# Attention with keys on the partitions, row maxima by a pass of their own, and fp32 probabilities times V

## The reference, cut to what matters

```
q, k, v = (h @ W).reshape(b, s, 16, 64)        # q and k rotated by position
logits  = einsum('bhqd,bhkd->bhqk', q, k)
logits  = where(causal, logits, -1e9) / 8
attn    = softmax(logits, axis=-1)
out     = einsum('bhqk,bhkd->bhqd', attn, v) @ Wo
x       = x + layernorm(out)
```

## Time and profile before

| | |
|---|---|
| median of 3 runs | 3296.17 us (3294.3 to 3298.45) |
| the profiled execution, its own time | 3296.03 us |
| its span, first to last instruction | 3294.2 us |
| PE busy | 2897.0 us (88%) |
| VectorE busy | 2390.9 us (73%) |
| ScalarE busy | 2022.5 us (61%) |
| GpSimd busy | 121.6 us (4%) |

### The profile page before, as it was taken

The page is one execution under the profiler, slowest core; times in us unless marked ns, Lnnn a source line. Parts: engine busy times, 40 slices in busy tenths (PEclk is TensorE's granted clock), DMA queues, the critical chain, the costliest instruction groups (busy, mean ns, idle before and its releaser), DMA issues. The chain is left out here.

```text
span 3294.2 us, 58839 instructions
## 1 busy us (share of the span) xinstructions
PE 2897.0 (88%) x17856; PEld 1547.4 (47%) x17856; DVE 2390.9 (73%) x4289; ACT 2022.5 (61%) x4003; POOL 121.6 (4%) x397
## 2 busy tenths in 40 slices
PE   4989999688888888985883699999999999999996
PEld 2534444466666666663441244444444444444442
DVE  6535555688888888884556787787777777777767
ACT  1114443688888888882214767676676676676742
POOL 0000000000000000000002000000000000000002
PEclk9999999899999999997996899999999999999998
DMA  4322222201010101102112111111111111111124
GB/s 164 116 77 58 76 76 64 72 22 40 22 41 22 40 22 35 27 5 86 64 70 69 53 52 49 50 52 52 46 52 49 50 52 45 53 46 52 52 71 153
DMA packets 77773, 188.88 MB, mean 57 GB/s; under 512 B 12304, under 2 KB 12688, under 8 KB 77200
## 3 DMA queue, kind: packets, MB, share of 16 engines
q1 hardware_dynamic: 77456, 185.13, 17.7%
HBM read 151.52 MB, written 33.55 MB: 56 GB/s over the span
## 5 line engine op out<-in xcount | busy, mean ns | idle before, releaser
L1234 PE MATMUL gp<-region,wgu 128*128 128x512 f16 x4224 | 931.3, 383 | 89.3 <-DVE wgu L1392 89.3
L1271 ACT ACTIVATE line<-code,offsets 128x512 f32<-128x512 f32 x1056 | 697.2, 713 | 111.3 <-DVE below L1370 45.7
L1234 PEld LDWEIGHTS gp<-region,wgu 128*128 128x128 f16 x4224 | 416.0, 99 | 600.9 <-issue 110.9
L786 ACT ACTIVATE probs<-logits,nbias,coef 128x512 f32<-128x512 f32 (+3 forms) x640 | 461.0, 720 | 100.4 <-POOL nbias L719 86.4
L1247 PE MATMUL yp<-wd,inter 128*128 128x512 f16 x2112 | 463.9, 380 | 24.5 <-DVE wd L1392 17.4
L835 DVE SCALAR_TENSOR_TENSOR pt_pair<-tp,pt_pair 128x512 f16<-128x512 f32 (+3 forms) x640 | 385.8, 603 | 76.2 <-ACT pt_pair L795 72.4
L736 PE MATMUL logits<-k_sb,q_sb 128*128 128x512 f16 (+3 forms) x1280 | 347.3, 354 | 104.6 <-ACT probs L786 61.2
L819 DVE TENSOR_REDUCE mx<-logits 128x1 f32<-128x512 f32 (+3 forms) x640 | 383.9, 600 | 33.7 <-PE logits L736 33.1
L795 ACT ACTIVATE pt_pair<-tp 128x512 f16<-128x512 f32 (+3 forms) x640 | 343.4, 537 | 25.2 <-PE tp L749 21.0
L749 PE MATMUL tp<-ident,probs 128*128 128x128 f32 x2176 | 349.2, 276 | 4.3 <-DVE pt_pair L835 2.7
L548 PE MATMUL pq<-region,wt_pair 128*128 128x512 f16 x1536 | 333.4, 380 | 14.9 <-DVE wt_pair L599 14.9
(11 more groups left out here) (107 smaller groups left out, 2823.0 us busy)
## 6 DMA issues: line engine op xcount, KB each, us to landing
qk_pairs<-r_pair SPq DMA_DIRECT2D x128, 128.0 KB, 2.1
k_sb<-qk_pairs SPq DMA_DIRECT2D x64, 256.0 KB, 5.4
cst<-in_gate_codes SPq DMA_DIRECT2D x44, 256.0 KB, 2.6
sst<-in_gate_scales SPq DMA_DIRECT2D x88, 128.0 KB, 2.9
cst<-in_up_codes SPq DMA_DIRECT2D x44, 256.0 KB, 2.7
sst<-in_up_scales SPq DMA_DIRECT2D x88, 128.0 KB, 3.1
cst<-in_down_codes SPq DMA_DIRECT2D x44, 256.0 KB, 2.7
sst<-in_down_scales SPq DMA_DIRECT2D x88, 128.0 KB, 3.0
```

Source lines behind the costliest of these rows:

```text
L786: a.activation(probs[:, g0 % P_RING, 0:w * P], sp_[:, g0 % S_RING, 0:w * P], ACT.Exp, bias=nbias[:, m:m + 1], scale=col(coef, 0), accum_ou ...
L1234: mm = pe.matmul(gp[:, e % 2, m, :], wgu[:, par, m, a, col0:col0 + P], xnT[:, b, k, tok], start=(k == 0 and a == b), stop=(k == KT - 1 and ...
L1271: a.activation(line[:, k % 4, :], code7[:, :], ACT.Identity, scale=slope, bias=offsets[:, k:k + 1]).then_inc(s_L.sem, 1)
```

## The change

Stages 1, 3 and 4 change.

- **Stage 1**: V is kept as one fp32 number. `v_hi` becomes `v_out`, which writes fp32 on ScalarE; `v_lo` is gone. A 65th column of ones stands beside the 64 of each head (`DV = D + 1`), set by one VectorE memset at the start of stage 3.
- **Stage 3** has two passes over a head. The first (`item`, `maximum`) makes the logits with queries on the partitions, with q_hi, q_lo and k_hi alone (one matmul a chunk in place of two), only for the maxima. When the 40 chunks of a head are through, one small reduce, one transpose, one ScalarE copy and two DMAs (to HBM, and from there to 64 partitions) put the negated maxima into rows 64 to 127 of `q2`. The second pass (`scores`, 27 slots behind the first) makes the logits with keys on the partitions, in groups of four pieces of 128 keys by 256 queries. Its second matmul holds k_lo in rows 0 to 63 and a constant in rows 64 to 127, so it also subtracts the maxima. ScalarE takes exp of a whole group (up to 1024 columns, no bias, no row sum). Two slots later `times_v` multiplies each 128x128 square of fp32 probabilities with 65 columns of fp32 V in one instruction; the ones column gives the row sum. VectorE divides each pair of output tiles by it. The turning of the squares, their hi and lo parts, GpSimd's bias and `o_lo` are gone. A head now has 20 groups and 20 slots.
- **Stage 4**: `on` is gone, and the transposes read `o_rows` itself. TensorE's list is written out instead of looped.

```
-        LAG_EXP, LAG_T, LAG_PV = 4, 6, 8
+        CHUNK = 2 * P
+        GROUP = 4 * CHUNK
+        for k in range(NI):
+            per_slot[k * (NGH - 1) // NI].append(k)
+        XLEAD, LAG_PV, P_RING = NGH + 7, 2, 4
...
+                def spread_max(t, u):
+                    sp.wait_ge(s_m.sem, s_m.done(t * 2 + u))
+                    sp.dma_start(m_dram[u], m16[:, u, :]).then_inc(d_ms.sems[u], 16)
+                    sp.wait_ge(d_ms.sems[u], d_ms.done(t + 1))
+                    sp.dma_start(q2[D:P, u, :], m_dram[u:u + 1].rearrange("a t p -> a (t p)").to_broadcast([D, S])
...
+                        pe.matmul(bank, k1[:, u, keys], q1[:, u, q0:q0 + w], start=True, stop=False)
+                        mm = pe.matmul(bank, k2[:, u, keys], q2[:, u, q0:q0 + w], start=False, stop=not diagonal)
...
+                    mm = pe.matmul(sx[:, b, 0:w], xq[:, u, qt * P:(qt + 1) * P], xk[:, u, c * CH:c * CH + w],
+                                   start=True, stop=not diagonal)
...
-                        pe.matmul(op[:, :], pt_pair[:, g0 % PT_RING, 0, at], v_at,
-                                  start=(kt == 0), stop=False)
-                        mm = pe.matmul(op[:, 0:D], pt_pair[:, g0 % PT_RING, 1, at], v_hi_at,
-                                       start=False, stop=(kt == qt))
+                            mm = pe.matmul(ob[:, m % 2, tile * CHUNK:tile * CHUNK + DV],
+                                           probs[:, n0(u, g) % P_RING, c0:c0 + P], v_at,
...
                 def slot(at):
+                    x, z, w = at(0), at(XLEAD), at(XLEAD + LAG_PV)
+                    if z:
+                        scores(*z)
+                    if x:
+                        t, u, q = x
+                        for k in per_slot[q]:
+                            item(t, u, k)
+                    if w:
+                        times_v(*w)
+                    if x and x[2] == NGH - 1:
+                        turn_max(x[0], x[1])
...
+                    a.activation(probs[:, n0(u, g) % P_RING, 0:w], st3[:, n0(u, g) % 2, 0:w], ACT.Exp,
+                                 scale=col(coef, 0)).then_inc(s_P.sem, 1)
...
+                        v.reciprocal(rinv[:, m % 2, :].unsqueeze(2), b[:, :, D:DV]).then_inc(s_rv.sem, 1)
+                        v.wait_ge(s_rv.sem, s_rv.done(tile))
+                        v.tensor_tensor(o_rows[:, 2 * m:2 * m + 2, bass.ds((t * 2 + u) * D, D)], b[:, :, 0:D],
...
-                def v_lo(i, u):
-                    v.wait_ge(s_vhi.sem, s_vhi.done(i))
...
-                    if st.has(2, ST):
-                        i = st.item(2)
-                        v.wait_ge(s_t4.sem, s_t4.room(i))
-                        v.tensor_tensor(on[:, :].rearrange("p (h d) -> p h d", d=D),
```

More of the change, by code:

```diff
@@ L28 @@
 SC = S // CH
+DV = D + 1
 GW = 2 * P
@@ L629, in build @@
         c2.close()
[L639 to L649, removed]
@@ L699, in _, with both, part, load_max @@
             def _(sp):
-                with sp.Fori(0, HEADS // 2) as t:
+                def both(which, head):
+                    return qk_dram[which, bass.ds(head, 1)].rearrange("a b r s -> (a b r) s")
+                def part(which, head, n):
+                    return qk_dram[which, bass.ds(head, 1), n].rearrange("a r s -> (a r) s")
+                def load_max(head, u):
+                    sp.dma_start(xq[:, u, :], both(0, head)).then_inc(d_X.sems[u], 16)
+                    for copy in range(2):
+                        sp.dma_start(xk[copy * D:(copy + 1) * D, u, :], part(1, head, 0)).then_inc(d_X.sems[u], 16)
@@ L722, in _ @@
             @block.tensor
             def _(pe):
-                for s in (s_QK, s_PT, s_PV):
+                for s in (s_S, s_PV):
                     pe.sem_inc(s.sem, s.credit)
-                def logits(t, g0, g):
-                    m, c = place[g0]
-                    (u, qt), w = tiles[m], width(m, c)
-                    if m % (NT // 2) == 0 and c == 0:
-                        pe.wait_ge(d_q.sems[u], d_q.done(t))
-                    pe.wait_ge(s_P.sem, s_P.room(g))
-                    bank = sp_[:, g0 % S_RING, 0:w * P]
-                    diagonal = c == chunks[m] - 1
-                    for part in range(2):
-                        mm = pe.matmul(bank, q_sb[:, u, qt * P:(qt + 1) * P],
-                                       k_sb[:, u, part, c * CH:c * CH + w * P],
-                                       start=(part == 0), stop=(part == 1 and not diagonal))
-                    if diagonal:
-                        mm = pe.matmul(sp_[:, g0 % S_RING, (w - 1) * P:w * P], ident_bf[:, :],
-                                       mask_bf[:, :], start=False, stop=True)
-                    mm.then_inc(s_QK.sem, 1)
@@ new lines, in turn_max, with times_v @@
+                def turn_max(t, u):
+                    head = t * 2 + u
+                    pe.wait_ge(s_nm.sem, s_nm.done(head))
+                    pe.transpose(sx[0:ST, (u * NX + NI) % 2, 0:P], nm[:, u, :], ident[:, :]).then_inc(s_T.sem, 1)
+                def times_v(t, u, g):
+                    m, first, last, pieces = groups3[g]
+                    n = (t * 2 + u) * NGH + g
+                    pe.wait_ge(s_P.sem, s_P.done(n))
+                    if first:
+                        pe.wait_ge(s_o.sem, s_o.room((t * 2 + u) * NQ + (NQ - 1 - m)))
+                    c0 = 0
+                    for kt, q0, w in pieces:
+                        v_at = v_rows[:, kt, bass.ds(t * 2 + u, 1), :].rearrange("p a c -> p (a c)")
+                        for j in range(w // P):
+                            tile = (q0 + j * P - m * CHUNK) // P
+                            mm = pe.matmul(ob[:, m % 2, tile * CHUNK:tile * CHUNK + DV],
+                                           probs[:, n0(u, g) % P_RING, c0:c0 + P], v_at,
+                                           start=(first and c0 == 0), stop=(kt == 2 * m + tile),
+                                           skip_group_check=True)
+                            c0 += P
@@ L809, in _ @@
+                for u in range(2):
+                    a.sem_inc(d_ms.sems[u], 16)
                 slots(a, slot)
@@ L853, in _ @@
+                def slot(at):
+                    x, w = at(0), at(XLEAD + LAG_PV)
+                    if x:
+                        t, u, q = x
+                        for k in per_slot[q]:
+                            maximum(t, u, k)
+                        if per_slot[q] and per_slot[q][-1] == NI - 1:
+                            row_maxima(t, u)
+                    if w:
+                        output(*w)
                 slots(v, slot)
```

335 lines of the change are left out of this document (168 added, 167 removed).

## The result

| | before | changed |
|---|---|---|
| median, us | 3296.14 (3294.3 to 3298.45, 4 runs) | 3340.28 (3337.0 to 3340.98, 4 runs) |
| profiled execution: span, us | 3294.2 | 3339.2 |
| ratio to before | | 1.0133, 95% 1.0119 to 1.0147 |

The change makes the kernel slower by 44 us, 1.3%, well outside the interval of the ratio. The prediction was 3067, its range 3040 to 3295. It missed both.

The account below looks back on a forecast made before the run. Stage 3 was taken as bound by the coupling of three nearly full engines, stages 1 and 5 by PE. 3296.0 - 205 (stage 3) - 4 (its first load) - 3.4 (stage 1) - 17 (stage 4) = 3067 us, range 3040 to 3295.

Parts of the forecast that it names:

- V is 2176 fp32 instructions of 65 columns, t each: Stage 3, TensorE: probabilities times V, with t the time per instruction, taken as 0.115 us, 250 us in all.
- Its half about passes: Stage 3, fp32 product with V: the 65 columns pass four times, 0.110 us per instruction.
- Its half about loads: Stage 3, fp32 product with V: two weight loads of 0.06 us each (0.12) are hidden beside the passes.
- The load sets the distance: Rival, stage 3: 0.109 us between transposes is the load's time; two loads give 0.218, 224 us more, 3291; chance 0.07.
- The start: Start of stage 3: 33 us until the first scores, in which PE works 11.4 and idles 21.
- the other matmuls with their waits: Stage 3 without V, behind its start: 395 us (386 of matmuls, less 11.4 at the start, plus 20 of waits).
- Loads not hidden (slower): Rival, stage 3: an fp32 instruction's loads can't overlap its matmuls; 0.236 us each, 263 us more, 3330; chance 0.12.
- The first L538: End of stage 1: without V's lower part in VectorE's way, the barrier to stage 2 opens 3.4 us earlier.
- The shorter first load: Start of stage 3: 1 MB for head 0's maxima comes first, about 6 us instead of 10, less by 4.
- Stage 4 gave 17.5 for 17: Stage 4: an instruction leaves VectorE's chain, which sets the period; less by 14.7 + 2.4 = 17 us.
- VectorE's waits in short groups: Stage 3, end of each head: PE waits for VectorE's two reduces and an output, some 1.3 us a head, 20 in all.
- if starts of L814 stand 0.2 us apart: Sign of a wrong prediction, stage 3: fp32 instructions with V starting 0.2 us apart, where 0.115 was assumed.

Follow-up runs that it names:

- the narrow transposes: Changed kernel with every fp32 square but the first of each group replaced by one fp32 transpose, 128 weight columns, 64 columns passing; V left out there: 3080.51 us.
- the interleaved order: Changed kernel with the scores' f16 matmuls and the fp32 squares of probabilities times V alternating in each slot of stage 3, nothing left out: 3288.05 us, ratio 0.9972.
- four products: Changed kernel with probabilities and V as single f16, lower parts left out, and each square's product taken four times: 3141.32 us, ratio 0.9529.
- one product: Changed kernel with probabilities and V as single f16, lower parts left out, and one f16 matmul per square: 2924.62 us, ratio 0.887.

## Why the prediction was wrong

**The step that failed** is the term "V is 2176 fp32 instructions of 65 columns, t each", with t = 0.115. Its half about passes was right (0.110 us per square). Its half about loads, "two loads of 0.06 lie beside it, since loads are hidden in the earlier trace rows", was wrong in size: a load is 0.112, twice what passes beside it, so it sets the distance. Measured t = 0.220, V 479.5 us instead of 250, 229.5 us more. The 0.06 was read rightly from a transpose, and the narrow transposes confirm it; it isn't the load of an fp32 matmul. The text said that no fp32 matmul but transposes stood in the trace, and still carried a number over the very difference.

**The rival that came true** was "The load sets the distance", at 0.218 and a chance of 0.07; the earlier trace rows had been counted against it, and against the rule of the Trainium skill that says the same. It gave 3291, the time came out at 3340. The 49 us between are the sum's other errors, measured apart in the changed kernel:

- *Turns of the loop*: 27.5 us in six gaps, nothing in the sum. In the kernel before, six turns of up to 3.0 us cost 16.7; here six waits cost 25.9, and 44 in the interleaved order.
- *The start*: 38.4 us to the first scores instead of 33, at a granted clock of 0.50, the 1.2 GHz level; PE had stood idle for 17 us before it.
- *The clock behind the turns*: the other matmuls with their waits take 407 us behind the start, 395 in the sum; 29 of them stand at the 1.2 GHz level and would take half at the other. That leaves nothing for waits that the sum had too low.
- *t itself*: 0.220 for 0.218, 5 us.

**"Loads not hidden (slower)"** named nearly the right time, 3330, by a mechanism that doesn't occur: with 130 columns passing, the distance is still 0.112, so load and pass lie side by side. A chance given to its figure would have been right by luck.

**What held.** The first L538 starts at 239.26 instead of 242.61, 3.3 for 3.4. The shorter first load gave 4.1 for 4. Stage 4 gave 17.5 for 17. VectorE's waits in short groups, 20 in the sum, came 28 times from 640 us on, 14.7 us of PE's idle time and 28.8 of its loads' (59.6 with the first head's). VectorE stayed under 420 us busy and ScalarE under 350 (386.75 + 31.83 and 319.64 + 0.27), and the spread maxima were never waited for in mid-head. The text's own sign of failure, "if starts of L814 stand 0.2 us apart", is what came, since it meant an instruction: 0.223.

## What to carry to other kernels

A matmul costs the larger of its pass and the load of the next weight, so with few moving columns it is the weight that one pays for: the kernel before loaded f16 and hid it, the changed one loads 128 fp32 columns twice for every 65 that pass. Before an f16 pair is swapped for fp32, compare per square: two halves at 0.112 against three f16 products at 0.029 each. And a duration taken from one kind of instruction (here a transpose) bounds another only once the difference between them has a price of its own.

## What the runs showed of the hardware

- By the load-bound reading, a matmul's recorded start isn't when its columns begin. In runs of 65 columns the second half's record starts 57 ns behind the first's, while its weight is still loading; loads begin when the matmul ahead truly begins. Starts of single records suggested the serial reading; only a change of the columns told them apart.
- A change of the weight's shape within a run, 128 to 64 columns or rows and back, costs some 0.25 us a group for both changes (0.205 us at the first narrow half alone). A square of half the columns saves 0.108, so on few squares nothing is gained.
- The granted clock sets loads too: at the 1.2 GHz level an fp32 half of 128 weight columns takes 0.213 us, 0.112 at 2.4 GHz. A wait of PE at a turn of the loop thus costs more than itself: behind each of the changed kernel's six the clock was at the lower level for a while, and the two kernels without such a wait show no such stretch.
- The turn of a loop costs PE 4.3 us on average in the changed kernel (978 matmul records a turn), 7.4 with the same number in the interleaved order, 2.8 in the kernel before (1008) and 6.4 with four products (1522). With one product (706) and with the transposes (746) no such wait is in the trace. The count alone doesn't set it; what does stays open.
